# A graph layer's weighted sum by destination: lists of 125 edges one at a time instead of in pairs

## What is computed

```
z = h @ W_func.T
e = leaky_relu(concat(z[src], z[dst], w) @ W_att.T)
e_exp = exp(e - segment_max(e, dst)[dst])
alpha = e_exp / segment_sum(e_exp, dst)[dst]
agg = segment_sum(alpha[:, None] * z[src], dst)
gnn = h + relu(where(deg > 0, h @ W_self.T + agg, h))
```

## Time and profile before

| | |
|---|---|
| median of 3 runs | 2450.26 us (2447.32 to 2450.47) |
| the profiled execution's own time | 2448.67 us |
| its span | 2446.9 us |
| mean granted clock of PE | 0.866 |
| busy: PE, DVE, ACT, POOL | 78%, 63%, 27%, 62% |
| gathers of the loop (L631) | 900, 1124.9 us busy |
| chain that ended last | PE 37%, POOL 23%, DVE 14%, issue 11% |

### The profile page before, as it was taken

The page is one execution under the profiler, slowest core; times in us unless marked ns, Lnnn a source line. Parts: engine busy times, 40 slices in busy tenths (PEclk is TensorE's granted clock), DMA queues, the critical chain, the costliest instruction groups (busy, mean ns, idle before and its releaser), DMA issues.

```text
span 2446.9 us, 38929 instructions
## 1 busy us (share of the span) xinstructions
PE 1910.1 (78%) x10986; PEld 1522.3 (62%) x10986; DVE 1551.7 (63%) x3673; ACT 649.9 (27%) x2743; POOL 1508.8 (62%) x1214
## 2 busy tenths in 40 slices
PE   5899677588877777778777777787875768999992
PEld 3555577477765665666665666566653447888882
DVE  7997799877765665665666566666654763236263
ACT  2444788431111111111111111111101333343330
POOL 2001555788888888887888888888881177225154
PEclk9999555599988898888888888988887878999996
DMA  9887988355444445544444444554456555447363
GB/s 225 256 243 216 329 291 291 106 128 154 128 124 124 124 124 135 145 125 128 124 126 123 125 124 123 138 143 126 123 125 199 150 159 156 127 117 195 104 188 98
DMA packets 317205, 384.74 MB, mean 157 GB/s; under 512 B 120296, under 2 KB 270542, under 8 KB 313996
## 3 DMA queue, kind: packets, MB, share of 16 engines
q1 hardware_dynamic: 175745, 240.35, 31.8%
q0 software_dynamic: 141376, 143.43, 24.0%
HBM read 291.32 MB, written 91.11 MB: 156 GB/s over the span
## 4 chain that ended last, share of the span: by engine, by line
PE 37%; POOL 23%; DVE 14%; issue 11%; DMA 6%; ACT 6%; DVEq 1%; SPq 1%; ACTq 0%; POOLq 0%
PE bank L670 36%; POOL wexp L631 22%; DMA wexp<-func_rows,a_src 4%; ACT work L1121 3%; DVE wexp L1505 1%; DVE wexp L1383 1%; PE bank L1001 1%; POOL g_all L657 1%; DMA wexp<-lr_d 1%; SPq L349 1%; DVEq L1542 1%; DVE work L1483 1%; DVE acc L1386 0%; DMA work<-in_wv 0%; DVE work L1773 0%
## 5 line engine op out<-in xcount | busy, mean ns | idle before, releaser
L631 POOL DMA_INDIRECT wexp<-func_rows,a_src x900 | 1124.9, 1250 | 274.1 <-issue 259.5
L670 PE MATMUL bank<-wexp,onehot 125*125 125x257 f32 x1800 | 545.8, 457 | 267.6 <-DMA wexp<-func_rows,a_src 173.1
L670 PEld LDWEIGHTS bank<-wexp,onehot 125*125 125x125 f32 x1800 | 392.0, 227 | 400.7 <-issue 298.2
L1721 DVE TENSOR_TENSOR acc<-bank,acc 125x257 f32 x450 | 190.8, 424 | 416.4 <-PE bank L670 386.1
L1709 DVE TENSOR_SCALAR onehot<-iota_r,a_rel,a_hi 125x125 f32<-125x125 f32 x900 | 292.0, 396 | 0.0
L597 POOL TENSOR_TENSOR work<-iota_h,a_hi 125x600 f32<-125x600 f32 x75 | 114.0, 1521 | 275.8 <-PE bank L703 193.2
L657 POOL DMA_INDIRECT g_all<-y_d,work x100 | 126.4, 1264 | 213.1 <-DMA y_d<-g_all 111.1
L670 PE MATMUL bank<-g_all 128*128 128x256 f32 x1040 | 238.3, 382 | 7.9 <-DVE g_all L1931 4.3
L670 PEld LDWEIGHTS bank<-g_all 128*128 128x128 f32 x1040 | 194.2, 192 | 33.4 <-issue 5.9
L670 PE MATMUL bank<-work,w_s 128*128 128x250 f32 x800 | 188.9, 378 | 27.9 <-ACT work L1148 27.1
L647 POOL DMA_INDIRECT sorted_d<-acc,work x100 | 121.4, 1214 | 135.1 <-DVE acc L1791 101.8
(11 more groups left out here) (277 smaller groups left out, 2775.5 us busy)
## 6 DMA issues: line engine op xcount, KB each, us to landing
wexp<-lr_d SPq DMA_DIRECT2D x75, 750.0 KB
wexp<-in_attr SPq DMA_DIRECT2D x25, 896.0 KB
g_all<-sorted_d SPq DMA_DIRECT2D x65, 256.0 KB
y_d<-g_all SPq DMA_DIRECT2D x65, 256.0 KB, 3.1
wexp<-func_rows,a_src POOLq DMA_INDIRECT x900, 3.9
sorted_d<-spare SPq DMA_DIRECT2D x48, 256.0 KB, 5.4
sorted_d<-spare SPq DMA_DIRECT2D x24, 384.0 KB, 4.6
work<-xn_rows SPq DMA_DIRECT2D x38, 224.0 KB
```

The lines of the kernel that those rows point to most:

```text
L631: pool.indirect_dma_start(ring[:, 2 * z + k, 0:D], None, func_rows, bass.IndirectOffsetOnAxis(ap=a_src[:, n // CS, j:j + 1], axis=0)).then ...
L670: return pe.matmul(o, l, r, start=first, stop=last_, **kw)
L1721: v.tensor_tensor(to, bank[3 + z % 2][0:R, 0:D + 1], to, ALU.add).then_inc(s("summed"), 1)
```

## The change

The unit becomes one list. There are 800 lists, STEPS is 850, and a turn has 34 steps of one gather and one product each. The rows of the table are 85 of 10 steps with 1250 edges. The table is found in another way: 8 comparisons of 850 elements on 100 partitions, and 80 matmuls of one column that add them. The fetches by indirect DMA are 20 and 10 instead of 12 and 6, at half the size. ACT sums eight columns of each row instead of ten. In the loop the ring keeps 34 slots in use, the gathers are counted in groups of six, one-hots are built 17 steps ahead, and the block numbers are loaded 12, 11 and 11 at a time. The steps on PE stand at new places (0, 1; 2, 3; 4 to 10; 11 to 14; 15 to 22; 23 to 33), and those of DVE's three `steps` are 0 to 11, 12 to 22 and 23 to 33. `body` on DVE is unchanged. The core of the diff:

```diff
-PAIRS = E // (2 * R)
-STEPS = 450
-QS, CS = 75, 6
-JS = 2 * CS
-LROW = CS * 2 * R
+LISTS = E // R
+KEYS = 8
+STEPS = 850
+QS, CS = 85, 10
+JH = CS // 2
+LROW = CS * R
...
-HS = ZS // CS
+HS = 3
+SUBS = ((0, 12), (12, 23), (23, ZS))
+AHEAD = ZS // 2
+SLOTS = 36
+TRIO = 6
+RIN = [min(TRIO, ZS - TRIO * k) for k in range(-(-ZS // TRIO))]
+LIN = [len([q for q in range(QS) if (q + 1) % HS == k]) for k in range(HS)]
...
-ON_ACT = 10
+ON_ACT = 8
...
-        ew_d = nc.dram_tensor("ew_d", (PAIRS, 2 * R), F32).ap()
+        ew_d = nc.dram_tensor("ew_d", (LISTS, R), F32).ap()
...
-        wexp = sb("wexp", [128, 2 * ZS * (D + 1)])
-        assert 3 * EXPERTS * 2 * D <= 2 * ZS * (D + 1)
+        wexp = sb("wexp", [128, SLOTS * (D + 1)])
...
-        onehot = sb("onehot", [R, 2 * CS, R], stack=place)
-        junk = onehot[:].rearrange("p a b -> p (a b)")
+        onehot = sb("onehot", [R, AHEAD, R], stack=place)
...
-                    pool.indirect_dma_start(d_[:, c * 2 * R:(c + 1) * 2 * R], None,
-                                            s_.rearrange("(t e) -> t e", e=2 * R), at).then_inc(s("sd_in"), 16)
+                    pool.indirect_dma_start(d_[:, c * R:(c + 1) * R], None,
+                                            s_.rearrange("(t e) -> t e", e=R), at).then_inc(s("sd_in"), 16)
...
                 freed(pool, s("stepped"), n - ZS + 1)
-                for k in range(2):
-                    j = 2 * (n % CS) + k
-                    pool.indirect_dma_start(ring[:, 2 * z + k, 0:D], None, func_rows,
-                                            bass.IndirectOffsetOnAxis(ap=a_src[:, n // CS, j:j + 1], axis=0)
-                                            ).then_inc(s(f"rows_in{z // 3}"), 16)
-
-            for n in range(ZS - 2):
-                step_rows(n)
-
-            for n in range(ZS - 2, STEPS):
+                pool.indirect_dma_start(ring[:, z, 0:D], None, func_rows,
+                                        bass.IndirectOffsetOnAxis(ap=a_src[:, n // CS, n % CS:n % CS + 1], axis=0)
+                                        ).then_inc(s(f"rows_in{z // TRIO}"), 16)
+
+            for n in range(STEPS):
...
-            mm(bank[1][0:QS, 0:PAIRS], ones_row[:, 0:QS], tab_t[:, 1, :], True, True).then_inc(s("tab_ps"), 1)
+            pe.wait_ge(s("consts"), 4)
+            for c in range(CS):
+                for k in range(KEYS):
+                    last = mm(bank[1][0:QS, c:c + 1], below[:, k, c::CS], ones_p[0:LISTS // KEYS, 0:1], k == 0, k == KEYS - 1)
+            last.then_inc(s("tab_ps"), 1)
...
-                    freed(pe, s("masked"), 4 * (q - HS + 1))
-                    for j in range(JS):
+                    freed(pe, s("masked"), 3 * (q - HS + 1))
+                    for j in range(CS):
                         for p in range(PART):
-                            mm(bank[1 + 2 * h + j // CS][:, (j % CS) * HIS:(j % CS + 1) * HIS],
+                            mm(bank[1 + 2 * h][:, j * HIS:(j + 1) * HIS],
                                lr_oh[h][0:R, j * R:j * R + 128], s1_p[:, p, :], p == 0, p == PART - 1)
-                    for j in range(JS):
-                        last = mm(bank[2 + 2 * h][:, CS * HIS + PART * j:CS * HIS + PART * (j + 1)],
+                    for j in range(CS):
+                        last = mm(bank[2 + 2 * h][:, PART * j:PART * (j + 1)],
                                   lr_oh[h][0:R, LROW + j * R:LROW + j * R + 128],
-                                  s2_p[:, bass.ds(q + j // 2 * QS, 1), :].rearrange("p a k -> p (a k)"), True, True)
+                                  s2_p[:, bass.ds(q + j * QS, 1), :].rearrange("p a k -> p (a k)"), True, True)
                     last.then_inc(s("lr_used"), 1)
 
             repeated(pe, QS // HS, body)
+            body(QS // HS, QS % HS)
...
                 n = i * ZS + z
-                pe.wait_ge(s(f"rows_in{z // 3}"), 96 * (i + 1))
-                pe.wait_ge(s("onehot"), 2 * n + 2)
+                pe.wait_ge(s(f"rows_in{z // TRIO}"), 16 * RIN[z // TRIO] * (i + 1))
+                pe.wait_ge(s("onehot"), n + 1)
                 freed(pe, s("summed"), n - 1)
-                for k in range(2):
-                    last = mm(bank[3 + z % 2][0:R, 0:D + 1], onehot[:, 2 * (z % CS) + k, :], ring[:, 2 * z + k, :],
-                              k == 0, k == 1)
-                last.then_inc(s("stepped"), 1)
+                mm(bank[3 + z % 2][0:R, 0:D + 1], onehot[:, z % AHEAD, :], ring[:, z, :], True, True).then_inc(s("stepped"), 1)
 
             def body(i, more=True):
                 if more:
                     queries(i + 1)
                 hidden(i, 0)
-                step(i, 0)
+                for z in range(2):
+                    step(i, z)
                 hidden(i, 1)
-                step(i, 1)
+                for z in range(2, 4):
+                    step(i, z)
                 hidden(i, 2)
-                for z in range(2, CS):
+                for z in range(4, 11):
                     step(i, z)
                 if more:
                     attention(i + 1)
                     self_part(i + 1)
                 hidden(i, 3)
-                step(i, CS)
-                step(i, CS + 1)
+                for z in range(11, 15):
+                    step(i, z)
                 down(i, 0)
-                for z in range(CS + 2, 2 * CS):
+                for z in range(15, 23):
                     step(i, z)
                 if more:
                     project(i + 1)
                 down(i, 1)
-                for z in range(2 * CS, 3 * CS):
+                for z in range(23, ZS):
                     step(i, z)
                 if more:
                     turn(i + 1)
...
-                for a in (1, 0):
-                    v.scalar_tensor_tensor(
-                        sel[:, h, a * CS * HIS:(a + 1) * CS * HIS].rearrange("p (j n) -> p j n", n=HIS),
-                        away[:, h, a * CS * HIS:(a + 1) * CS * HIS].rearrange("p (j n) -> p j n", n=HIS), 0.0,
-                        bank[1 + 2 * h + a][0:R, 0:CS * HIS].rearrange("p (j n) -> p j n", n=HIS),
-                        ALU.is_equal, ALU.mult).then_inc(s("masked"), 1)
+                v.scalar_tensor_tensor(sel[:, h, :], away[:, h, :], 0.0, bank[1 + 2 * h][0:R, 0:CS * HIS], ALU.is_equal,
+                                       ALU.mult).then_inc(s("masked"), 1)
                 freed(v, s("selected"), n - HS + 1)
-                v.tensor_reduce(a_s[:, h, 1, :], bank[2 + 2 * h][0:R, CS * HIS:CS * HIS + PART * JS]
+                v.tensor_reduce(bank[0][0:R, h * CS:(h + 1) * CS], bank[2 + 2 * h][0:R, 0:PART * CS]
...
-            def blocks_of(q):
+            def blocks_of(n, count):
                 _, values = nc.values_load_multi_w_load_instructions(
-                    blk_row[:, bass.ds(q * CS, CS)], engines=[mybir.EngineType.DVE], min_val=0, max_val=BLOCKS - 1,
+                    blk_row[:, bass.ds(n, count)], engines=[mybir.EngineType.DVE], min_val=0, max_val=BLOCKS - 1,
...
             def one_hot(i, z):
-                q = i * HS + z // CS
-                for k in range(2):
-                    at = lambda a: a[:, bass.ds(q, 1), 2 * (z % CS) + k:2 * (z % CS) + k + 1].rearrange("p a b -> p (a b)")
-                    v.tensor_scalar(onehot[:, 2 * (z % CS) + k, :], iota_r[:], at(a_rel), at(a_p), ALU.is_equal,
-                                    ALU.mult).then_inc(s("onehot"), 1)
+                at = lambda a: flat(a)[:, bass.ds(i * ZS + z, 1)]
+                v.tensor_scalar(onehot[:, z % AHEAD, :], iota_r[:], at(a_rel), at(a_p), ALU.is_equal, ALU.mult).then_inc(s("onehot"), 1)
 
             def steps(i, h):
 
-                at = blocks_of(i * HS + h)
-                for c in range(CS):
-                    z = h * CS + c
+                z0, z1 = SUBS[h]
+                at = blocks_of(i * ZS + z0, z1 - z0)
+                for z in range(z0, z1):
                     n = i * ZS + z
                     v.wait_ge(s("stepped"), n + 1)
                     freed(v, s("summed"), n)
-                    to = accv[:, bass.ds(at[c], 1), :].rearrange("p b n -> p (b n)")
+                    to = accv[:, bass.ds(at[z - z0], 1), :].rearrange("p b n -> p (b n)")
                     v.tensor_tensor(to, bank[3 + z % 2][0:R, 0:D + 1], to, ALU.add).then_inc(s("summed"), 1)
-                    if h + 1 < HS:
-                        one_hot(i, z + CS)
+                    if z + AHEAD < ZS:
+                        one_hot(i, z + AHEAD)
                     elif not (isinstance(i, int) and i == GROUPS - 1):
-                        one_hot(i + 1, c)
+                        one_hot(i + 1, z + AHEAD - ZS)
```

More of the change, by code:

```diff
@@ L225, in build @@
         l_self = sb("l_self", [R, 2, D])[:]
-        tab_t = w(0, [1, 2, PAIRS], 2)
-        away, sel = w(6, [R, HS, JS * HIS], 4), w(10, [R, HS, JS * HIS], 4)
+        iota_n = w(0, [LISTS // KEYS, STEPS], 2)
```

(29 more changed lines are left out.)

116 lines of the change are left out of this document (62 added, 54 removed).

## The result

The changed kernel takes 2748.3 us (median of 4 runs, 2745.7 to 2752.1) beside 2450.4 us of the kernel before: ratio 1.122, 95% interval 1.1207 to 1.1233. The forecast was 2608 with a range up to 2700. The direction and the reason were right. The size was not: the loop's turn grew by more than the terms of the sum allowed. The profiled execution took 2745.67 us, with a span of 2743.6.

What follows compares the result with a forecast made beforehand. The prediction took POOL's gathers to bound the kernel before, and DVE's adds and PE after the change. From 2448.7 us, it added 165.6 for the loop and took off 6 for other stages: 2608 us, range 2480 to 2700.

Steps and rivals of the forecast that it cites:

- the loads: DVE's register loads of block numbers: 16 more values cost 1.5 us a turn, with ends 0 and 3.1.
- (b): Turn from `attention` to `down(0)`: m_attention waits behind step 11's add, PE idles nearly 6 us; 14.70 us.
- (c): Turn from `down(0)` to `project`: `down(0)`, a clock loss of 1.65 and eight steps; 9.94 us.
- (d): Turn from `project` to the add of step 12: unchanged at 8.28 us.
- (f): Turn from the last step's add to the next first add, with layer norms and register load: 11.10 us.
- (a): Turn from its first add to `attention`: 9.44 us, of which 1.65 for the clock.
- (e): Turn from the add of step 12 to the last step's add: ten steps, 5 x 1.32 = 6.60 us.
- the 77.7 us: Time on POOL that 50 fewer gathers at 1.5545 us would take away: the gain on offer, forecast as worth nothing.
- rival 2: Attention still overlaps in the loop and PE keeps its clock: 7.0 us a turn less, 2440; chance 0.05.
- Pace of a burst: Steps in bursts on PE and DVE: one list ties up a bank for 1.32 us, 0.66 a list with two banks.
- Rival 3: PE's clock holds in the loop and register loads are free: 4.8 us less a turn, 2491; chance 0.15.
- Rival 4: Longer tails: 2.05 us more in (f) and 1.6 more for loads in proportion each turn, 2696; chance 0.12.

Runs made afterwards that it cites:

- run 4: Run 3 with hidden(1) and hidden(2) on PE no longer behind steps that wait for adds: 2393.0 us, ratio 0.978.
- run 5: Changed kernel with two lists put into one bank and one DVE add for both, leaving out 425 of 850 adds: 2436.8 us, ratio 0.994.
- run 1: Changed kernel with DVE's first bundle ending one step earlier, so m_attention stands behind the add of step 10: 2602.0 us, ratio 1.063.
- run 2: Changed kernel with block numbers padded so each register load starts at a multiple of 16 bytes: 2646.2 us, ratio 1.081.
- run 3: Changed kernel with the edits of run 1 and run 2 together: 2440.0 us, ratio 0.997.
- run 6: Run 5 with the add for each pair of lists made twice, so all 850 adds are back: 2535.5 us, ratio 1.036.
- run 7: Changed kernel with idle products on PE before its three long waits of a turn: 2681.2 us, ratio 1.094.
- run 8: Kernel before the change, with DVE's m_attention behind the add of step 6 instead of ahead of it: 2451.2 us, ratio 0.999.
- e6_all: Run 4 plus one add for two lists, with the same 425 adds left out as in run 5: 2373.0 us, ratio 0.968.

## Where the prediction was right, and where it failed

The forecast by its own parts, beside the mean of 24 turns. Its 1.5 us for the loads stood apart. What the loads cost is read from the start of the instruction ahead of a first add (0.68 us long) to that add: 2.33 in (b, c), 2.88 in (d) and 3.64 in (f). In the turn of the earlier trace rows the same three, each the idle time in brackets and 0.68 or 0.69 for the instruction ahead, are 1.77, 2.20 and 1.26, so they grew by 3.6 us.

| part | forecast | measured | difference | of it loads | rest |
|---|---|---|---|---|---|
| a | 9.44 | 9.86 | +0.42 | | +0.42 |
| b and c | 24.64 | 26.01 | +1.37 | +0.56 | +0.81 |
| d | 8.28 | 9.71 | +1.43 | +0.68 | +0.75 |
| e | 6.60 | 8.27 | +1.67 | | +1.67 |
| f | 11.10 | 13.49 | +2.39 | +2.38 | +0.01 |
| loads | 1.5 | | -1.5 | | |
| turn | 61.56 | 67.35 | +5.8 | | |

24 turns x 5.8 = 139 us. The profiled execution is 2745.7 - 2608 = 138 us above the forecast, and the earlier stages gave 4 us more than forecast: the loop explains the miss within 3 us.

- *What bounds it.* Right: gathers stopped being the bound, DVE's adds and PE took their place, and the 77.7 us were worth nothing. Runs 4 and 5 show the bound coming back once the rest is shorter.
- *The order in (b).* Right in place, and near in size. Forecast for (b) and (c) 24.64, of which rival 2 called 7.0 us avoidable; run 1 gave back 6.0 a turn with bad loads, and 8.7 between runs 2 and 3 with good ones.
- *Pace of a burst.* Forecast 0.66 us a list; adds in a burst stand 0.64 to 0.75 apart. Run 6 bears out the reasoning behind it, that banks are tied up rather than DVE short of time.
- **The register loads failed.** This is the first term that was mis-sized: "by that slope, 0.093 a value, 16 more values are 1.5 us a turn", with 3.1 as its end. They cost 3.6, so 2.1 us a turn or 51 us were missing here. The slope came from two medians, and a median of loads with mixed starts hides what sets them. The earlier trace rows had the warning: six values took 810 ns at best and 2365 at worst. The 1.158 us is no typical load at all, only the longest of the 38 aligned ones beside 37 of 1.40 and more. In the kernel before a turn's loads start 72 bytes after the last turn's, now 136, so the places alternate in both. The Trainium skill (Runtime: NRT & Kernel Launch, section on instruction fetch mechanics) gives about 200 ns a register; unaligned loads of 11 values agree, at 2.53 us (230 ns each), but aligned ones of 12 took 0.86 (72 ns each). The 193 ns each of the forecast's six-value row, which seemed to agree, come from that same median: the aligned half took 137 ns a value, the other half 237. The 3.2 us a turn by the Trainium skill was nearer to the 3.6 than my 1.5.
- **The clock in (e) failed.** The second: (e) was priced at 5 x 1.32 with full clock, though its text put a load and DVE's layer norm ahead of it, and PE's idle there is 4.1 us, as good as the 3.82 us of the earlier trace rows after which the clock was 0.54. I charged the clock in (a) and (c) and forgot the third stop. (e) is 1.67 us a turn longer, 40 us in all. Run 7 shows the cause for 1.2 of the 1.67: with the stop filled, (e) is 7.07.
- *The rest*, +2.0 us a turn, 48 in all. 0.75 of it is in (d), where two steps of the layer norm, L1326 and L1568, took 0.53 and 1.13 us in every turn; in the early turn from which the forecast cut its parts the same two took 0.17 and 0.74. One turn was too few to read a part from. The 0.8 us in (b) and (c) and the 0.4 in (a) were not traced to a cause.
- *Rival 3* (full clock, free loads: 2491) was off the wrong way on both counts. *Rival 4* (longer tails and loads in proportion: 2696) had the right direction with half of the reason: (f) without its load was as forecast, and the loads grew by 3.6 us, past the 3.1 of proportion. The range ended at that rival, whose end for the loads was too low and which had no term for the clock in (e).
- *Other stages.* Forecast -6, measured -10.1. The look-up's rows span 196.8 us for 202.4, which is the forecast's -6, though the comparison of 2500 elements took 1.254 us and not 0.86, so that its length is not what sets the row. What stands between the last of them and the first add gave 5.6 us where the forecast had 2, so that the -6 for the look-up came out by sizes that were not its own.

```profile
L1523 DVE TENSOR_SCALAR wexp<-wexp,iota_p 128x2500 bf16<-128x2500 bf16 x85 | 106.5, 1254 | 12.9 <-DMA wexp<-lr_d 12.6
```

## What to carry to other kernels

When a change cuts work on the bounding engine, ask what a turn would be without that engine, and then walk the next engine's in-order queue: an instruction that moves one place past a dependence can be the largest term of a change (run 1). Ask as well what stands behind the wait that it causes: the late `m_attention` of run 8 was harmless in a kernel with slack under its gathers, where nothing large was queued behind a waiting step. Where two engines hand work over through a few buffers, count how much of the work each buffer holds; halving what a bank holds halves the lead of the producer, and in the changed kernel's order that cost twice what the extra adds did (runs 5 and 6), while with the order and the loads mended both together were worth 20 us (e6_all). And fill or shorten the long stops of PE in a turn, since part of each is paid again in slower products behind it (run 7).

## What was not expected of the hardware

- A register load from SBUF depends on where it starts more than on its length: 12 values from a multiple of 16 bytes took 0.86 us, 11 from such a place 1.3, 11 from elsewhere 2.5 to 2.6, 12 from elsewhere 2.7 to 3.3 (the middle load of run 1). Six values took 0.82 from such a place and 1.42 from elsewhere. Why 12 aligned values are faster than 11 was not tried; 12 is a multiple of four.
- Transfers slow an unaligned load of 12 values (5.1 to 6.0 us at the head of a turn, and 3.5 to 3.9 with the zero fills away), while the aligned load of 12 at the same place stayed at 0.87 us. An aligned load of 11 there took 1.3 us in some kernels and up to 4.1 in e6_all.
- Idle products on PE made a kernel 67 us faster in which PE was already busy 74% of the span.
